# Weighed keys ahead of the next scores: TensorE's order in each step of a streamed attention

## The chip, the cores and the metric

The kernel is written in Bass and runs on one core of a Trainium2 chip. The metric is the device time of one execution in microseconds. All five engines (PE is TensorE, DVE is VectorE, ACT is ScalarE, POOL is GpSimd, SP is SyncE) run their own instruction streams and meet only in semaphores.

## The reference

Three layers with residuals on x of 2 x 256 rows of 512. The change lies in the first, a cross attention of 16 heads over 4096 keys of width 128 in each of the two batches:

```python
x = x + xattn(layernorm(x), ctx_512, ...)     # touched by the change
x = x + attn(layernorm(x), ...)
x = x + ffn(layernorm(x), ...)

# in xattn; kv_r is ctx_512 after rope, one set of keys for all heads of a batch
scores = jnp.einsum('bhsr,bhlr->bhsl', q_r, k_r)
attn = jax.nn.softmax(scores, axis=-1)
ctx_c = jnp.einsum('bhsl,bld->bhsd', attn, kv_r)
```

## The kernel before

**Tiling.** Weights are first folded into the queries, so a query of 128 columns meets the turned keys directly. The attention runs over 64 tiles of queries (2 batches, 16 heads, 2 tiles of 128 rows, `NQT`); each tile meets the 4096 keys in four chunks of 1024 (`NCH`), so there are 256 chunks (`NCHUNK`). To keep float32's precision each operand is split in a high and a low part.

**The life of chunk n.**

- PE, `scores(n)`: six matmuls of 512 columns (lines 1152 to 1154) into one of three slots in PSUM (`slot`, `RING` = 3; two in `ps_s`, one in `ps_t`). `free_slot` waits until the exponents of chunk n-3 have been read out. The last matmul raises `s_done`.
- DVE, `chunk_maximum(n)` (line 864): waits for `s_done`, one maximum over 1024 scores.
- ACT, `exponents(n)` (line 606), then `take_hi(n)` (line 597): exponents in float32, then their high part as float16 into `p_both`; `take_hi` waits for the landing of chunk n-3, whose buffer it takes.
- DVE, `take_lo(n)` (line 856): the low part.
- SP, `turn_exponents(n)` (lines 339 and 340): waits for the end of the weighed keys of chunk n-3 (`pv_done`, the target's buffer) and for `lo_done`, then issues one transposing DMA of both parts (512 KB) from `p_both` to `pt_both`, which raises `pt_in`.
- PE, `weighed_keys(n)`: waits for `pt_in`, then 24 matmuls of 128 columns (lines 1180, 1181, 1184) into `ps_o`.
- DVE, once for each tile: `row_maximum` (line 872) and `weigh_chunks` (line 887), which reads `ps_o`; POOL makes the weights, sums the chunks and splits the next query (`split_query`, lines 444 and 446).

**What sets the order.** Each engine's order is written out by hand. PE does scores 0 to 3 first (`AHEAD` = 4) and then goes through its loop at line 1224. DVE's loop is, for each n: `weigh_chunks` of the tile before (at every fourth n), `chunk_maximum(n + 1)`, `take_lo(n)`, `row_maximum` (at every fourth). ACT's is `exponents(n)`, `take_hi(n)`. SP issues the transposes in order, with a load of later weights (`wmix`) between them once for each 8 chunks of the second half. An engine that waits holds everything behind it in its own stream.

**The turn of the keys.** Batch 1 has other keys. In the four steps ahead of it PE's `next_keys` turns a chunk of 1024 keys through the same three slots (line 1163), and ACT and DVE copy its high and low parts to `kt_hi` and `kt_lo` (lines 612 and 878), in place of the keys of batch 0.

Of the kernel before, what the change touches and what calls it, by code (L numbers as in the profile page):

```python
# [59 lines left out]
def build(nc, x, ctx_kv, wq_t, w_kcq, w_qr_t, w_kr_t, w_kckv, wo_t, cos_q, sin_q, cos_k, sin_k,  # L60
          w_mix, w_gu, w_dn, s_gu, s_dn, out):
    with ExitStack() as stack:
# [969 lines left out]
        def _(pe):  # L1032
# [108 lines left out]
            def scores(n):  # L1141

                k, t, c = RING_AT["chunk", n], n // NCH, n % NCH
                free_slot(k)
                if c == 0:
                    pe.wait_ge(q_ready, t + 1)
                if t % (NQT // B) == 0:
                    pe.wait_ge(kt_done, 8 * (t // (NQT // B)) + 2 * (c + 1))
                for a in range(2):
                    o = slot(k)[:, a, :]  # L1150
                    cols = slice(c * CHUNK + a * HALF, c * CHUNK + (a + 1) * HALF)
                    nc.tensor.matmul(o, q_hi[:, t % 2, :], kt_hi[:, cols], start=True, stop=False)  # L1152
                    nc.tensor.matmul(o, q_hi[:, t % 2, :], kt_lo[:, cols], start=False, stop=False)  # L1153
                    last = nc.tensor.matmul(o, q_lo[:, t % 2, :], kt_hi[:, cols], start=False, stop=True)  # L1154
                last.then_inc(s_done, 1)

            def next_keys(c):

                k = RING_AT["keys", c]
                free_slot(k)  # L1160
                for j in range(CHUNK // P):
                    blk = c * (CHUNK // P) + j
                    last = nc.tensor.transpose(slot(k)[:, j // 4, j % 4 * P:(j % 4 + 1) * P],
                                               kvr[:, 1, blk * P:(blk + 1) * P], ident[:, :])
                last.then_inc(ktt_done, 1)

            def weighed_keys(n):
                b, t, c = n // (NCHUNK // B), n // NCH, n % NCH
                if c == 0 and t >= 2:
                    pe.wait_ge(o_used, t - 1)  # L1170
                if n < NCH:
                    pe.wait_ge(kn_done, 2 * (n + 1))
                elif n == NCHUNK // B:
                    pe.wait_ge(kn_done, KN_DONE)
                o = ps_o[:, t % 2, c * P:(c + 1) * P]
                pe.wait_ge(pt_in[n % RING], 16 * (n // RING + 1))
                pt_hi, pt_lo = pt_both[:, n % RING, 0], pt_both[:, n % RING, 1]
                for k in range(CHUNK // P):
                    keys = slice((c * (CHUNK // P) + k) * P, (c * (CHUNK // P) + k + 1) * P)
                    nc.tensor.matmul(o, pt_hi[:, k, :], kn_hi[b][:, keys], start=(k == 0), stop=False)  # L1180
                    nc.tensor.matmul(o, pt_hi[:, k, :], kn_lo[b][:, keys], start=False, stop=False)  # L1181
                for k in range(CHUNK // P):
                    keys = slice((c * (CHUNK // P) + k) * P, (c * (CHUNK // P) + k + 1) * P)
                    last = nc.tensor.matmul(o, pt_lo[:, k, :], kn_hi[b][:, keys], start=False,  # L1184
                                            stop=(k == CHUNK // P - 1))
                last.then_inc(pv_done, 1)
# [35 lines left out]
            pe.wait_ge(qabs_ok, H)  # L1222
            pe.wait_ge(d_ok, H)
            for n in range(NCHUNK):
                if n + AHEAD < NCHUNK:
                    scores(n + AHEAD)
                if ("keys", n + AHEAD - NCHUNK // B + NCH) in RING_AT:
                    next_keys(n + AHEAD - NCHUNK // B + NCH)
                weighed_keys(n)


            def turn_norm(kind, t):
# [168 lines left out]
```

## Time and profile before

| | us |
|---|---|
| median of 3 runs | 1244.73 |
| lowest and highest | 1244.6, 1246.05 |
| the profiled execution | 1240.12 |
| its span, first to last instruction | 1238.3 |
| PE busy | 1114.0 (90%) |
| DVE busy | 985.4 (80%) |
| ACT busy | 704.3 (57%) |
| POOL busy | 578.0 (47%) |

The span is what the views of the trace divide up; the profiled execution's own time is 1.8 us longer. PE's busy time counts matmuls, which overlap: the end of a row on PE is modelled, and the next matmul starts ahead of it. The distance between starts is therefore the time that a matmul costs. "PEld" is PE's loading of weights. A DMA's start is that of the issuing instruction on SP, and its landing is the last of its 16 engines' signals.

### The profile page before, as it was taken

The numbers are of one execution on the slowest core, as the hardware profiler recorded it, in microseconds if no ns is written. First come the engines' busy times: TensorE is split into PE (matmuls) and PEld (weight loads), VectorE is DVE, ScalarE is ACT, GpSimd is POOL, SyncE is SP. The second block draws the span as 40 slices with busy tenths as digits, with TensorE's granted clock in tenths as the row PEclk, the third lists the DMA queues.
The fourth block names the chain that finished last, engine by engine and source line by source line (L and its number), as shares of the span: only waits on it lengthen the run. The fifth ranks groups of instructions, "written<-read, shape, count | busy, mean of one in ns | idle before, by whom it ended". The sixth has DMA issues, their size and how long they took to land.

```text
span 1238.3 us, 23318 instructions
## 1 busy us (share of the span) xinstructions
PE 1114.0 (90%) x9080; PEld 838.0 (68%) x9080; DVE 985.4 (80%) x930; ACT 704.3 (57%) x1029; POOL 578.0 (47%) x698
## 2 busy tenths in 40 slices
PE   4999997999999999998999999999998869875688
PEld 3555556888888878876787788778787334334567
DVE  4887777899889989887888888888886089996933
ACT  1223236788878878876777777777775031113321
POOL 1993351765766444433344344343442077885200
PEclk9999998999999999999999999999999889987889
DMA  8443305999999999998999999999999200040000
GB/s 303 140 145 99 97 22 105 179 190 183 186 184 191 188 174 190 183 184 163 184 198 186 192 192 196 184 186 191 184 191 163 102 1 0 1 186 1 1 18 17
DMA packets 553990, 175.78 MB, mean 142 GB/s; under 512 B 535072, under 2 KB 541216, under 8 KB 553760
## 3 DMA queue, kind: packets, MB, share of 16 engines
q1 hardware_dynamic: 552272, 169.14, 73.4%
q10 hardware_dynamic: 1616, 5.24, 1.2%
q8 instruction: 69, 1.13, 0.4%
q14 instruction: 33, 0.27, 0.1%
HBM read 39.07 MB, written 1.05 MB: 32 GB/s over the span
## 4 chain that ended last, share of the span: by engine, by line
PE 64%; DMA 19%; DVE 8%; issue 4%; POOL 4%; ACT 2%; DVEq 0%; POOLq 0%; ACTq 0%; SPq 0%
DMA pt_both<-p_both 19%; PE ps_o L1180 7%; PE ps_o L1181 7%; PE ps_o L1184 6%; PE ps_s L1152 5%; PE ps_s L1153 4%; PE ps_s L1154 4%; PE ps_o L1214 3%; PE ps_o L1085 3%; PE ps_s L1060 3%; PE ps_t L1152 2%; POOL prod L517 2%; PE ps_s L1244 2%; PE ps_t L1153 2%; PE ps_t L1154 2%
## 5 line engine op out<-in xcount | busy, mean ns | idle before, releaser
L856 DVE SCALAR_TENSOR_TENSOR p_both<-prob,p_both 128x1024 f16<-128x1024 f32 x256 | 326.4, 1275 | 18.2 <-ACT p_both L597 17.7
L597 ACT ACTIVATE p_both<-prob 128x1024 f16<-128x1024 f32 x256 | 270.6, 1057 | 55.4 <-DMA pt_both<-p_both 37.0
L1180 PE MATMUL ps_o<-kn_hi,pt_both 128*128 128x128 f16 x2048 | 259.0, 220 | 31.6 <-DMA pt_both<-p_both 29.9
L1180 PEld LDWEIGHTS ps_o<-kn_hi,pt_both 128*128 128x128 f16 x2048 | 194.2, 98 | 107.1 <-issue 60.6
L1181 PE MATMUL ps_o<-kn_lo,pt_both 128*128 128x128 f16 x2048 | 256.7, 219 | 0.0
L864 DVE TENSOR_REDUCE nmax<-ps_s 128x1 f32<-128x1024 f32 x172 | 210.2, 1222 | 54.6 <-PE ps_s L1154 52.7
L606 ACT ACTIVATE prob<-ps_s,nmax 128x1024 f32<-128x1024 f32 x172 | 191.7, 1114 | 77.5 <-DVE nmax L864 77.0
L1181 PEld LDWEIGHTS ps_o<-kn_lo,pt_both 128*128 128x128 f16 x2048 | 201.2, 98 | 0.0
L1184 PE MATMUL ps_o<-kn_hi,pt_both 128*128 128x128 f16 x2048 | 156.6, 219 | 0.0
L1152 PE MATMUL ps_s<-kt_hi,q_hi 128*128 128x512 f32 x344 | 150.4, 437 | 4.9 <-DVE kt_lo L878 2.8
L1154 PE MATMUL ps_s<-kt_hi,q_lo 128*128 128x512 f32 x344 | 136.5, 397 | 0.0
L1153 PE MATMUL ps_s<-kt_lo,q_hi 128*128 128x512 f32 x344 | 134.3, 390 | 0.0
L444 POOL CAST q_hi<-arena 128x128 fp32r<-128x128 f32 x64 | 18.8, 293 | 230.2 <-PE ps_s L1154 160.5
L1184 PEld LDWEIGHTS ps_o<-kn_hi,pt_both 128*128 128x128 f16 x2048 | 125.5, 98 | 0.0
L864 DVE TENSOR_REDUCE nmax<-ps_t 128x1 f32<-128x1024 f32 x84 | 102.7, 1223 | 26.3 <-PE ps_t L1154 25.3
L606 ACT ACTIVATE prob<-ps_t,nmax 128x1024 f32<-128x1024 f32 x84 | 93.6, 1114 | 36.5 <-DVE nmax L864 36.3
L469 POOL TENSOR_TENSOR osum<-oscl 128x256 f32<-128x256 f32 x64 | 46.4, 726 | 135.0 <-DVE oscl L887 135.0
L1154 PEld LDWEIGHTS ps_s<-kt_hi,q_lo 128*128 128x128 f32 x344 | 64.8, 188 | 15.2
L1152 PE MATMUL ps_t<-kt_hi,q_hi 128*128 128x512 f32 x168 | 73.5, 438 | 1.4 <-DVE kt_lo L878 1.4
L1152 PEld LDWEIGHTS ps_s<-kt_hi,q_hi 128*128 128x128 f32 x344 | 65.3, 190 | 12.8 <-DVE kt_lo L878 3.2
L453 POOL TENSOR_TENSOR junk<-alpha,rsum 128x4 f32<-128x4 f32 x64 | 65.7, 1027 | 11.6 <-ACT alpha L617 6.6
L1153 PEld LDWEIGHTS ps_s<-kt_lo,q_hi 128*128 128x128 f32 x344 | 65.8, 191 | 7.6
(129 smaller groups left out, 2004.4 us busy)
## 6 DMA issues: line engine op xcount, KB each, us to landing
wgu_raw<-w_gu_dram SPq DMA_DIRECT2D x11, 512.0 KB, 7.5
wq_s<-wq_t_dram SPq DMA_DIRECT2D x16, 256.0 KB, 3.6
wot_s<-wo_t_dram SPq DMA_DIRECT2D x16, 256.0 KB, 2.8
kvr<-ctx_kv_dram ACTq DMA_DIRECT2D x4, 1024.0 KB, 13.7
pt_both<-p_both SPq DMA_TRANSPOSE x256, 4.6
kvr<-w_mix_dram SPq DMA_DIRECT2D x16, 256.0 KB, 3.4
wkcq_s<-w_kcq_dram SPq DMA_DIRECT2D x16, 192.0 KB, 3.0
wdn_raw<-w_dn_dram SPq DMA_DIRECT2D x1, 2816.0 KB, 9.1
```

The lines of the kernel that those rows point to most:

```text
L453: nc.gpsimd.tensor_tensor(junk[:, i, :], alpha[:, i, :], rsum[:, i, :], ALU.mult).then_inc(row_ok, 1)
L469: nc.gpsimd.tensor_tensor(osum[:, :, :], oscl[:, i, 0:2, :], oscl[:, i, 2:4, :], ALU.add).then_inc(ctx_half, 1)
L597: nc.scalar.mul(p_hi(n), prob[:, n % 2, :], PSCALE).then_inc(hi_done, 1)
L606: nc.scalar.activation(prob[:, n % 2, :], scored, ACT.Exp, bias=nmax[:, i, c:c + 1], scale=1.0, accum_out=rsum[:, i, c:c + 1]).then_inc(ex ...
L856: nc.vector.scalar_tensor_tensor(out=p_lo(n), in0=prob[:, n % 2, :], scalar=PSCALE, in1=p_hi(n), op0=ALU.mult, op1=ALU.subtract).then_inc( ...
L864: nc.vector.tensor_reduce(nmax[:, i, c:c + 1], flat(slot(RING_AT["chunk", n])), AX_X, ALU.max, negate=True).then_inc(m_done, 1)
L1152: nc.tensor.matmul(o, q_hi[:, t % 2, :], kt_hi[:, cols], start=True, stop=False)
L1153: nc.tensor.matmul(o, q_hi[:, t % 2, :], kt_lo[:, cols], start=False, stop=False)
L1154: last = nc.tensor.matmul(o, q_lo[:, t % 2, :], kt_hi[:, cols], start=False, stop=True)
L1180: nc.tensor.matmul(o, pt_hi[:, k, :], kn_hi[b][:, keys], start=(k == 0), stop=False)
L1181: nc.tensor.matmul(o, pt_hi[:, k, :], kn_lo[b][:, keys], start=False, stop=False)
L1184: last = nc.tensor.matmul(o, pt_lo[:, k, :], kn_hi[b][:, keys], start=False, stop=(k == CHUNK // P - 1))
```

## The change

In PE's loop over the chunks the call of `weighed_keys(n)` moves from the end of the step to its beginning, ahead of the scores of chunk n+4 and, in the four steps that have them, ahead of the turned keys. Nothing else differs; the waits inside each function stay as they are.

```diff
--- before.py
+++ after.py
@@ -1222,11 +1222,11 @@
             pe.wait_ge(qabs_ok, H)
             pe.wait_ge(d_ok, H)
             for n in range(NCHUNK):
+                weighed_keys(n)
                 if n + AHEAD < NCHUNK:
                     scores(n + AHEAD)
                 if ("keys", n + AHEAD - NCHUNK // B + NCH) in RING_AT:
                     next_keys(n + AHEAD - NCHUNK // B + NCH)
-                weighed_keys(n)
 
 
             def turn_norm(kind, t):
```

## Rows read from the trace of the kernel before

**Rows 1.** The page: busy us (share of the span) xinstructions of each engine.

```profile
PE 1114.0 (90%) x9080; PEld 838.0 (68%) x9080; DVE 985.4 (80%) x930; ACT 704.3 (57%) x1029; POOL 578.0 (47%) x698
```

**Rows 2.** Windows by stage; the columns stand in the first line.

```profile
core 0: us, PE busy (x) PEld busy (x) DVE busy (x) ACT busy (x) POOL busy (x), PEclk, DMA share, GB/s
202.50:956.90 754.40, 722.03 (x7684) 603.15 (x7685) 653.79 (x635) 583.57 (x825) 352.74 (x592) 1.00 1.09 186
```

**Rows 3.** Timeline of PE, 608 to 612 us: start, length, engine, line, operation, count.

```profile
608.42 0.23 PE L1180 MATMUL ps_o<-kn_hi,pt_both 128*128 128x128 f16 x1 [1.12 <-DMA pt_both<-p_both]
...
609.74 0.48 PE L1152 MATMUL ps_t<-kt_hi,q_hi 128*128 128x512 f32 x1
...
610.98 0.40 PE L1154 MATMUL ps_t<-kt_hi,q_lo 128*128 128x512 f32 x1
611.22 0.23 PE L1180 MATMUL ps_o<-kn_hi,pt_both 128*128 128x128 f16 x1
```

**Rows 4.** Waits, 202.5 to 956.2 us, PE and SP's queue: total us, times, longest.

```profile
PE ps_o L1180 <- DMA pt_both<-p_both: 29.9, 37, 3.5
...
SPq L340 <- PE ps_o L1184: 353.2, 231, 2.7
```

**Rows 5.** The chain that ended last, 608 to 633 us: start, us, what.

```profile
613.85 6.35 DMA pt_both<-p_both
620.24 0.23 PE ps_o L1180
...
626.03 6.08 DMA pt_both<-p_both
632.15 0.23 PE ps_o L1180
```

**Rows 6.** Timeline of DVE, 611 to 619 us.

```profile
611.42 1.23 DVE L864 TENSOR_REDUCE nmax<-ps_t 128x1 f32<-128x1024 f32 x1 [0.71 <-PE ps_t L1154]
612.56 1.22 DVE L856 SCALAR_TENSOR_TENSOR p_both<-prob,p_both 128x1024 f16<-128x1024 f32 x1
...
615.35 1.22 DVE L856 SCALAR_TENSOR_TENSOR p_both<-prob,p_both 128x1024 f16<-128x1024 f32 x1
...
618.28 1.46 DVE L856 SCALAR_TENSOR_TENSOR p_both<-prob,p_both 128x1024 f16<-128x1024 f32 x1
```

**Rows 7.** DMA, 202.5 to 956.2 us: queue packets; issues, KB, median us to landing.

```profile
q8 instruction: 60, 0.98, 0.5%
...
pt_both<-p_both SPq DMA_TRANSPOSE x254, 4.6
```

**Rows 8.** DMA, three short windows: from 610.6, from 641.5, from 654.1 us.

```profile
pt_both<-p_both SPq DMA_TRANSPOSE x1, 4.2
...
q8 instruction: 1, 0.02, 4.1%
...
pt_both<-p_both SPq DMA_TRANSPOSE x1, 5.2
...
q8 instruction: 1, 0.02, 11.8%
...
pt_both<-p_both SPq DMA_TRANSPOSE x1, 5.7
```

**Rows 9.** Timeline of PE where the keys turn, 553 to 566 us.

```profile
554.85 0.50 PE L1152 MATMUL ps_t<-kt_hi,q_hi 128*128 128x512 f32 x1 [1.37 <-DVE kt_lo L878]
...
565.39 0.50 PE L1152 MATMUL ps_s<-kt_hi,q_hi 128*128 128x512 f32 x1 [1.44 <-DVE kt_lo L878]
```

**Rows 10.** Windows: 1.5 us behind a landing that came late.

```profile
608.20:609.70 1.50, 1.28 (x23) 1.29 (x24) 0.57 (x2) 1.31 (x2) 0.75 (x2) 1.00 1.24 280
```

**Rows 11.** Windows of two waits of PE, and the end of the second.

```profile
202.90:206.30 3.40, 3.40 (x25) 3.11 (x23) 1.61 (x2) 2.92 (x5) 2.17 (x5) 0.50 1.14 210
583.80:586.80 3.00, 0.01 (x1) 0.00 (x0) 1.23 (x1) 0.02 (x1) 0.00 (x0) 1.00 1.20 218
...
586.81 0.23 PE L1180 MATMUL ps_o<-kn_hi,pt_both 128*128 128x128 f16 x1 [3.00 <-DMA pt_both<-p_both]
```

## The prediction

> **What bounds the kernel now.** I write S(n) for the scores of chunk n (six matmuls) and W(n) for its weighed keys (24 matmuls); there are 256 chunks. The engine table comes first [rows 1]: PE is busy 90% of the span, so one looks for the stretch where it is not. The table by stage puts the change inside one stretch, 202.5 to 956.9 us [rows 2]: 754.4 us, from the start of W(0) to the end of W(255). Less the last W's 1.5 us that is 752.9 us for 255 steps, 2.95 us each. The rest of the kernel is not touched.
>
> PE's own order of time shows what a step costs [rows 3]: W starts at 608.42, the next S at 609.74, the next W at 611.22. W takes 1.32 us, S 1.48 us, together 2.80 us. So 0.15 us of a step is waiting, and the PE waits name the transposing DMA of the exponents, 29.9 us in 37 waits [rows 4]. The chain shows how: a DMA of 6.35 us from 613.85, W at 620.24, then a DMA of 6.08 us and W at 632.15 [rows 5]. With W(137) at 608.42 that is one late landing every 11.8 to 11.9 us, four chunks.
>
> What closes this circle is VectorE's written order: maximum of chunk n+1, then the low half of chunk n. With n = 141: W(137) starts at 608.42; S(142) comes behind it and ends at 610.98 + 0.40 = 611.38, which is 2.96 us later; the maximum of 142 starts at 611.42; the low half of 141 must stand behind it, starts at 612.56 and takes 1.22; the DMA of 141 starts at 613.85 and lands after 6.35; W(141) starts at 620.24 [rows 3, 5, 6]. The sum is 2.96 + 0.04 + 1.14 + 1.22 + 0.07 + 6.35 + 0.04 = 11.82 us, all of the distance. **The circle runs over four chunks because S(n+1) stands behind W(n-4) on PE.**
>
> The DMA of 6.35 us is not the usual one. The median landing takes 4.6 us, and an unhindered one 4.2 us [rows 7, 8]. In this stretch queue 8, instructions, brings 60 packets of 16 KB [rows 7]; PE starts 7684 + 7685 instructions there [rows 2], which is 256 for a packet, one packet each 4.2 chunks (255 / 60). Where a packet falls into a transpose the landing took 5.2 us at 642 and 5.7 us at 654 [rows 8], and the DMAs of 6.35 and 6.08 us meet one late in their flight. I take these as landings held up by an instruction fetch.
>
> **The change part by part.** No instruction, byte or buffer is added or taken away, and PE still needs 2.80 us a step. Only the order moves. Before: S(n+4), W(n). After: W(n), S(n+4), and in the four steps with keys W, S, then the eight transposes of the keys. So every S, and the transposes of keys with it, is now queued behind one more wait for a landing. In terms of circles each loses one chunk of lead: S(n+1) stands behind W(n-3), not W(n-4), and S(n) behind W(n-4), not W(n-5).
>
> Circle one, through VectorE's order, without a fetch: 2.96 + 0.04 + 1.14, the low half 1.28 (three of four take 1.22, the fourth 1.46, [rows 6]), 0.07, a landing of 4.35 (between 4.2 and the median 4.6, nearer the unhindered row, since DMAs will start farther apart), 0.04. That is 9.88 us, now over **three** chunks: 3.29 us a step. Before it was spread over four, 2.47, and bound only with a fetch in it.
>
> Circle two, through the chunk's own work: 2.96 from W to the end of S; from there to the end of the low half 5.19 (S(142) ends at 611.38, its low half at 615.35 + 1.22 = 616.57, [rows 3, 6]), 5.28 on average with the 0.34 us that the fourth chunk has more (0.24 of it the longer low half, 0.10 estimated for its wait behind VectorE's scaling step); 0.07 + 4.35 + 0.04. Sum 12.70 us over four chunks, 3.18 a step without a fetch. But a fetch comes each 4.2 chunks, so this circle can meet nearly all of them. Over 21 chunks lie five fetches: five rounds of 12.70 and one plain PE step of 2.80 give 66.3 us plus five delays.
>
> The delay of a fetch: the rows give 5.2 - 4.35 = 0.85 us when it comes about 2 us into the transpose, 5.7 - 4.35 = 1.35 us later in it, and 6.35 - 4.35 = 2.0 us near its end [rows 5, 8]. The packets come one to two us behind a W's start. After the change a W starts as its own data lands, the next landing is 3.4 us off, so the next DMA was issued 4.35 - 3.4 = 0.95 us before this W: the packet then meets it some 2 to 3 us into its flight. I take the middle of the two rows for that, 1.1 us. (66.3 + 5.5) / 21 = **3.42 us a step**, above both bare circles.
>
> Tested on the kernel before, the same arithmetic gives five rounds of 11.87 and one step, 62.2 / 21 = 2.96, against 2.95 measured.
>
> The turn of the keys: for four chunks an S comes only each 5.3 us (554.85 and 565.39 are two apart, [rows 9]), since keys and scores share three slots. Resource and interval stay, so these four cost 4 x (5.3 - 3.42) = 7.5 us on top of the average after, where they cost 9.4 before.
>
> Sum: 255 x 3.42 + 7.5 = 879.6 us for the stretch, against 752.9: **+126.7 us**. The profiled execution of before took 1240.12 us with a span of 1238.3, and the median of its three runs is 1244.73. So 1366.8 for an execution like the profiled one, and 1371.4 against the median, which I predict.
>
> What else is moved past: W(n) now ends 1.48 us earlier against its S, which frees a buffer of transposed exponents for SP's queue and the accumulator for VectorE. Neither is late: W(138) ends at 611.22 + 1.32 = 612.54, and the DMA that needs its buffer starts only at 613.85, on the low half [rows 3, 5]. With less lead it has still more room. GpSimd's split of the next queries waits for scores and is needed four chunks on; it idles most of the stretch (352.7 of 754.4 us busy, [rows 2]). These cost nothing, and if GpSimd's cover were gone, at most 1.3 us once per four chunks.
>
> **The rivals.** *The fetch is hidden* (the longer step leaves time to catch up): circle one alone, 255 x 3.29 + 8 = 847, +94, **1339 us**. For it: behind a held landing the queue moved 280 GB/s where the stretch had 186 [rows 2, 10], so it can catch up. Against: W(141) and W(145) waited just for such landings. [...]
>
> *Every fetch costs its full 2.0 us*: (66.3 + 10) / 21 = 3.63, +180, **1425 us**.
>
> *The clock falls.* PE will idle 3.42 - 2.80 = 0.6 us a step, 2.6 us a round. [...] Against: behind a wait of 3.00 us at 586.81 the clock stayed 1.00 [rows 11], and my waits are shorter. [...]
>
> *Not slower: the buffer decides.* SP waited 353.2 us in 231 waits for the end of a W before it could issue a transpose [rows 4]. If these released the late DMAs, W ahead of S would issue each 1.48 us sooner and end the 29.9 us of PE's waits: **1215 us**. It decides only where W(n-3) ends later than the low half of n; at 612.54 against 613.78 it doesn't.
>
> *No change: the DMA engines are full.* At a share of 1.09 [rows 2] the order of PE would not matter: **1245 us**. Against: the 280 GB/s of [rows 10] and landings of 4.2 us.
>
> **How the numbers follow.** Forecast 0.70, fetch hidden 0.12, full delay 0.06, clock 0.05, DMA full 0.04, buffer 0.03. Slower by over 0.2%, about what a measurement of this kernel can tell, is then 0.93, same 0.04, faster 0.03. The range takes in the forecast, the hidden fetch with a landing 0.1 us shorter (-9 us) and nearly all of the full delay: 1328 to 1422.
>
> **What would show it.** Right: the stretch from first to last W near 880 us; before nearly each W a wait for the DMA, on PE some 150 us; VectorE's maxima waiting for PE more, its low halves starting 1.14 us behind the next maximum; SP released by the low half instead of W; unhindered landings at 4.2 to 4.5 us; granted clock 1.00. Wrong: landings at a median above 4.6 (the DMA term), a clock of 0.5 in the stretch, or PE's waits unchanged near 30 us, which would mean that the lead was not what bound.

## The result

The changed kernel takes **1411.16 us** in the median of 4 runs (1405.19 to 1415.83) against 1244.66 of the kernel before: a ratio of 1.1337, 95% interval 1.1284 to 1.1391. The forecast of 1371.4 had the way and the mechanism, and the time lies inside its range; the increase was +166.5 us where the sum had +126.7.

The page of the changed kernel, engines and the chain that ended last:

```profile
span 1406.1 us, 23318 instructions
...
PE 1142.8 (81%) x9080; PEld 850.1 (60%) x9080; DVE 979.5 (70%) x930; ACT 707.2 (50%) x1029; POOL 539.7 (38%) x698
...
PE 44%; DMA 30%; DVE 14%; issue 6%; POOL 3%; ACT 1%; SPq 0%; DVEq 0%; POOLq 0%; ACTq 0%
DMA pt_both<-p_both 30%; PE ps_o L1180 5%; DVE p_both L856 4%; PE ps_o L1181 4%; PE ps_o L1184 4%; DVE nmax L864 4%; PE ps_o L1214 3%; PE ps_s L1152 3%; PE ps_o L1085 3%; PE ps_s L1060 3%; PE ps_s L1153 2%; PE ps_s L1154 2%; POOL prod L517 2%; PE ps_s L1244 2%; PE ps_t L1152 1%
```

PE is busy 28.8 us more, though it issues the same instructions; DVE and POOL are busy less, ACT 2.9 us more [rows 1]. The chain of the kernel before had these shares:

```profile
PE 64%; DMA 19%; DVE 8%; issue 4%; POOL 4%; ACT 2%; DVEq 0%; POOLq 0%; ACTq 0%; SPq 0%
```

In the chain the transposing DMA has risen from 19% to 30% of a longer span, and DVE from 8% to 14%, with the low half (L856) and the maximum (L864) at 4% each.

The window from the start of W(0) to the end of W(255), with the columns of [rows 2]; the waits below it are to be read beside [rows 4]:

```profile
202.10:1125.90 923.80, 755.38 (x7690) 618.68 (x7690) 647.58 (x635) 586.41 (x825) 314.21 (x592) 0.98 0.87 152
```

What PE's weighed keys waited for there, us in total, times, longest:

```profile
PE ps_o L1180 <- DMA pt_both<-p_both: 169.9, 129, 5.8
```

And SP's queue, at line 339 for the low half and at line 340 for the buffer:

```profile
SPq L339 <- DVE p_both L856: 329.4, 226, 5.0
SPq L340 <- PE ps_o L1184: 167.2, 138, 3.6
```

The stretch grew from 754.4 to 923.8 us; less the last W it is 922.3 against 752.9 us, +169.4. The two profiled executions took 1407.89 and 1240.12 us, +167.8, so all of the increase lies in the stretch, 3.62 us a step instead of 2.95. PE's wait for landings went from 29.9 us to 169.9 us. SP's queue turned round: it waited 353.2 us for the end of a W and 103.8 for the low half before, and now waits 329.4 for the low half and 167.2 for a W. The buffer did come free earlier, and none of the transposes on the chain waited for it: each was issued behind its low half.

The chain inside the stretch, start, us, what. Each "PE ps_o L1180" of 0.23 us is the start of a W:

```profile
722.27 0.23 PE ps_o L1180
...
725.27 1.23 DVE nmax L864
726.50 1.14 DVE p_both L856
727.71 5.73 DMA pt_both<-p_both
733.48 0.23 PE ps_o L1180
...
736.45 0.07 PE ps_o L1180
...
739.28 1.22 DVE nmax L864
740.50 1.14 DVE p_both L856
741.71 5.87 DMA pt_both<-p_both
747.62 0.23 PE ps_o L1180
```

From 722.27 to 733.48 one sees circle one as the prediction drew it: W(n-3), the S behind it up to 725.27, the maximum, the low half, the DMA, W(n), three chunks in 11.21 us. From 733.48 to 747.62 the chain first takes one plain PE step (the W at 736.45) and then the same circle: four chunks in 14.14 us. Both DMAs, 5.73 and 5.87 us, are held landings.

### The profile page after: what moved, and what is told of

Same layout as the page of the kernel before. It is cut to its first block, busy times and chain, and to the rows that moved or that the text cites. A ratio compares the mean times of both kernels' runs of the same rounds, so it can differ in the third digit from the quotient of the medians.

```text
span 1406.1 us, 23318 instructions
## 1 busy us (share of the span) xinstructions
PE 1142.8 (81%) x9080; PEld 850.1 (60%) x9080; DVE 979.5 (70%) x930; ACT 707.2 (50%) x1029; POOL 539.7 (38%) x698
## 4 chain that ended last, share of the span: by engine, by line
PE 44%; DMA 30%; DVE 14%; issue 6%; POOL 3%; ACT 1%; SPq 0%; DVEq 0%; POOLq 0%; ACTq 0%
DMA pt_both<-p_both 30%; PE ps_o L1180 5%; DVE p_both L856 4%; PE ps_o L1181 4%; PE ps_o L1184 4%; DVE nmax L864 4%; PE ps_o L1214 3%; PE ps_s L1152 3%; PE ps_o L1085 3%; PE ps_s L1060 3%; PE ps_s L1153 2%; PE ps_s L1154 2%; POOL prod L517 2%; PE ps_s L1244 2%; PE ps_t L1152 1%
## 5 line engine op out<-in xcount | busy, mean ns | idle before, releaser
L1180 PE MATMUL ps_o<-kn_hi,pt_both 128*128 128x128 f16 x2048 | 262.7, 222 | 170.1 <-DMA pt_both<-p_both 169.9
L1180 PEld LDWEIGHTS ps_o<-kn_hi,pt_both 128*128 128x128 f16 x2048 | 196.7, 99 | 260.4 <-DMA pt_both<-p_both 170.8
L864 DVE TENSOR_REDUCE nmax<-ps_s 128x1 f32<-128x1024 f32 x172 | 210.4, 1223 | 191.3 <-PE ps_s L1154 190.9
L856 DVE SCALAR_TENSOR_TENSOR p_both<-prob,p_both 128x1024 f16<-128x1024 f32 x256 | 319.6, 1248 | 1.9 <-ACT p_both L597 1.8
L606 ACT ACTIVATE prob<-ps_s,nmax 128x1024 f32<-128x1024 f32 x172 | 191.9, 1116 | 215.2 <-DVE nmax L864 215.2
L1181 PE MATMUL ps_o<-kn_lo,pt_both 128*128 128x128 f16 x2048 | 260.6, 221 | 0.0
L444 POOL CAST q_hi<-arena 128x128 fp32r<-128x128 f32 x64 | 18.9, 295 | 419.1 <-PE ps_s L1154 296.3
L1184 PE MATMUL ps_o<-kn_hi,pt_both 128*128 128x128 f16 x2048 | 160.0, 222 | 0.0
L864 DVE TENSOR_REDUCE nmax<-ps_t 128x1 f32<-128x1024 f32 x84 | 102.7, 1223 | 80.3 <-PE ps_t L1154 79.9
L1152 PE MATMUL ps_s<-kt_hi,q_hi 128*128 128x512 f32 x344 | 154.8, 450 | 4.3 <-DVE kt_lo L878 2.8
L606 ACT ACTIVATE prob<-ps_t,nmax 128x1024 f32<-128x1024 f32 x84 | 93.7, 1116 | 93.4 <-DVE nmax L864 93.4
L1154 PE MATMUL ps_s<-kt_hi,q_lo 128*128 128x512 f32 x344 | 139.4, 405 | 0.0
L1153 PE MATMUL ps_s<-kt_lo,q_hi 128*128 128x512 f32 x344 | 138.0, 401 | 0.0
L1184 PEld LDWEIGHTS ps_o<-kn_hi,pt_both 128*128 128x128 f16 x2048 | 128.4, 100 | 0.0
L1154 PE MATMUL ps_t<-kt_hi,q_lo 128*128 128x512 f32 x168 | 67.0, 399 | 0.0
```

The source lines that it names most:

```text
L606: nc.scalar.activation(prob[:, n % 2, :], scored, ACT.Exp, bias=nmax[:, i, c:c + 1], scale=1.0, accum_out=rsum[:, i, c:c + 1]).then_inc(ex ...
L856: nc.vector.scalar_tensor_tensor(out=p_lo(n), in0=prob[:, n % 2, :], scalar=PSCALE, in1=p_hi(n), op0=ALU.mult, op1=ALU.subtract).then_inc( ...
L864: nc.vector.tensor_reduce(nmax[:, i, c:c + 1], flat(slot(RING_AT["chunk", n])), AX_X, ALU.max, negate=True).then_inc(m_done, 1)
```

## The experiments

In order of what they tell apart. "W first" and "S first" are the orders of the changed kernel and of the one before.

**1. Is it the order or the lead?** W first, with the scores five ahead:

```diff
-AHEAD = 4
+AHEAD = 5
```

> The changed order (weighed keys first), with the scores five chunks ahead instead of four. PE's stream is then chunk by chunk the one of the kernel before. If the lead between scores and weighed keys is what the change cost, the time is that of before, 1245 us (ratio 1.00). If putting a waiting W ahead of S costs by itself (the wait for a landing now stands at the head of the step), it stays near 1411 us.

Measured 1244.51 us, ratio 1.0006 (0.9993 to 1.0019). PE's stream is then the old one again, the turned keys included, so this run shows that the change is nothing else than one chunk of lead taken. What the lead is worth, and on which circle, it can't tell; experiments 2 to 4 and 6 can.

**2. Circle one alone.** PE's order as before, VectorE's maximum two chunks ahead of the low half:

```diff
+taken = 1
 for n in range(NCHUNK):
     ...                                # weigh_chunks, as before
-    if n + 1 < NCHUNK:
-        chunk_maximum(n + 1)
+    two = 1 if NCHUNK // B - NCH - 2 <= n < NCHUNK // B else 2
+    while taken < min(n + 1 + two, NCHUNK):
+        chunk_maximum(taken)
+        taken += 1
     take_lo(n)
```

> PE's order is that of the kernel before; VectorE takes the maximum two chunks ahead of the low half instead of one (one ahead only where the keys turn). Low half n then stands behind S(n+2), which stands behind W(n-3): circle one over three chunks, as in the changed kernel, while the chunk's own path keeps its five chunks of lead (12.70 / 5 = 2.54 us a step, not binding). If circle one is what costs in the changed kernel, this one comes near it: 1371 us by the sum of the prediction, 1411 us as the changed kernel measured. If the lead counts through the chunk's own path, it stays at 1245 us.

Measured 1409.24 us, ratio 1.1328 (1.1301 to 1.1356), the changed kernel's time within the intervals, on PE's old stream. Its page, the costliest PE group (L1183 is L1180 there) and the maximum:

```profile
L1183 PE MATMUL ps_o<-kn_hi,pt_both 128*128 128x128 f16 x2048 | 262.5, 222 | 169.6 <-DMA pt_both<-p_both 169.1
...
L864 DVE TENSOR_REDUCE nmax<-ps_s 128x1 f32<-128x1024 f32 x172 | 210.5, 1224 | 180.1 <-PE ps_s L1157 179.5
```

PE waits 169.1 us for landings, as in the changed kernel (169.9). VectorE's order and PE's order make the same circle, and a chunk of lead taken from it on either side costs the same. This also rules out the chunk's own path, which kept its five chunks here.

**3. Circle two.** The changed kernel with a shorter ScalarE instruction, in circle two and not in circle one:

```diff
-nc.scalar.activation(prob[:, n % 2, :], scored, ACT.Exp, ...)
+m = CHUNK if n < 2 else HALF
+nc.scalar.activation(prob[:, n % 2, 0:m], scored[:, 0:m], ACT.Exp, ...)
```

> The changed kernel; from chunk 2 on the exponents are taken of 512 of the 1024 columns only (the other half keeps old values, so the output is not the attention's). That shortens ScalarE's instruction by about 0.5 us in the chunk's own path (circle two) and leaves circle one alone. If circle two carries the time, a step shortens by 0.5 / 4.2 = 0.12 us, 255 steps 30 us: 1381 us. If circle one carries it, 1411 us, no change.

Measured 1415.45 us, ratio 1.1399 (1.1377 to 1.1421): not shorter at all. ScalarE's larger group of exponents, in the changed kernel (first, from its page) and in this one (in the stretch):

```profile
L606 ACT ACTIVATE prob<-ps_s,nmax 128x1024 f32<-128x1024 f32 x172 | 191.9, 1116 | 215.2 <-DVE nmax L864 215.2
...
L607 ACT ACTIVATE prob<-ps_s,nmax 128x512 f32<-128x512 f32 x169 | 116.2, 688 | 272.5 <-DVE nmax L865 272.5
```

The instruction did shrink, from 1116 to 688 ns, and ScalarE waits for the maximum that much longer.

**4. The low half, which stands in circle one** (and in circle two):

```diff
+m = CHUNK if n < RING else HALF
-nc.vector.scalar_tensor_tensor(out=p_lo(n), in0=prob[:, n % 2, :], ...)
+nc.vector.scalar_tensor_tensor(out=p_lo(n)[:, 0:m], in0=prob[:, n % 2, 0:m], ...)
```

> The changed kernel; from chunk 3 on VectorE takes the low part of 512 of the 1024 columns only (the other half keeps old values, so the output is a little off the attention's). The low half stands in circle one. It gets about 0.6 us shorter, and the chain of the changed kernel passes it 70 times: up to 42 us less, 1369 us. If VectorE's part does not carry the time, it stays at 1411 us, as it did with half the exponents.

Measured 1364.85 us, ratio 1.0961 (1.0931 to 1.0992), 46 us under the changed kernel where 42 were expected. VectorE's group:

```profile
L857 DVE SCALAR_TENSOR_TENSOR p_both<-prob,p_both 128x512 f16<-128x512 f32 x253 | 175.3, 693 | 1.2 <-ACT p_both L597 1.2
```

693 ns instead of 1248: 0.56 us taken from VectorE come back 46 / 0.56 = 83 times over 256 chunks. That is more than the 70 times that the chain passes the low half; in this run the clock also fell less often, four times in the stretch against 11 (the clock's cost is worked out in the next part). ScalarE's 0.43 us came back not once. The two together say that the circle that binds goes through VectorE and past the exponents.

**5. The fetches.** Six wide matmuls in place of 24 narrow ones, in both kernels:

```diff
-for k in range(CHUNK // P):            # 8 x (high, low keys), then 8 more
-    keys = ...
-    nc.tensor.matmul(o, pt_hi[:, k, :], kn_hi[b][:, keys], ...)
-    nc.tensor.matmul(o, pt_hi[:, k, :], kn_lo[b][:, keys], ...)
...
+for j in range(6):
+    keys = slice(c * CHUNK + j % 2 * HALF, c * CHUNK + (j % 2 + 1) * HALF)
+    pt = pt_hi if j < 4 else pt_lo
+    last = nc.tensor.matmul(ps_o[:, t % 2, :], pt[:, j, :], kn_hi[b][:, keys], ...)
```

> The changed kernel; each W's 24 matmuls of 128 columns are replaced by 6 of 512 columns (the same 3072 columns through PE, 24 instructions a chunk instead of 60; the output is not the attention's). W's own time stays near 1.3 to 1.4 us, but PE reads its instructions in 24 packets instead of 60. If the landings held up by instruction fetches are a term of the step, the excess of the landings on the chain (about 75 us in the changed kernel) shrinks to some 30 us: 1411 - 45 + 5 = 1371 us. If the late landings have another cause, it stays at 1411 to 1416 us.

> The same replacement in the kernel before. PE's step is then 2.80 to 2.87 us and 24 fetches are left. If fetches cause the late landings that PE waits for, its 0.15 us of waiting a step goes to under 0.06: 255 x 2.90 = 740 us for the stretch, 12 us less, about 1230 us. If not, 1245 us, or 1260 us by the longer W.

Measured 1364.57 us (ratio 1.0942, 1.0901 to 1.0983) and 1221.53 us (0.9807, 0.9765 to 0.9848). The queue of instructions in the stretch of the first:

```profile
q8 instruction: 25, 0.41, 0.2%
```

PE starts 3078 + 3079 instructions in that stretch (202.0 to 1081.5 us), which is 246 for a packet of 16 KB. In the changed kernel's stretch 7690 + 7690 starts meet 61 packets, 252 for each, so the packets follow PE's instructions down.

And three starts on its PE, S, W, S:

```profile
600.67 0.58 PE L1152 MATMUL ps_s<-kt_hi,q_hi 128*128 128x512 f32 x1
...
602.25 1.47 PE L1181 MATMUL ps_o<-kn_hi,pt_both 128*128 128x512 f16 x6
603.36 0.58 PE L1152 MATMUL ps_t<-kt_hi,q_hi 128*128 128x512 f32 x1
```

From S to S lie 603.36 - 600.67 = 2.69 us, so PE's step got 0.11 us shorter, where I had expected an equal W or a longer one. By estimate that alone is worth 0.11 x 114 = 13 us on the chain of the changed kernel (the 114 is worked out below), which leaves 34 of the 47 us to the fetches and to a clock that fell six times in the stretch instead of 11. In the kernel before, the chain passes W and S 119 times, in this run 161 times, so the shorter step is worth 13 to 18 of the 23 us and 5 to 10 are left to the fetches, against the expected 12; the run alone can't part them.

**6. One more chunk of lead, and one less.** S first with `AHEAD = 5`, and W first with `AHEAD = 3`:

> The kernel before with the scores five ahead instead of four (one more chunk of lead). Circle one then runs over five chunks: with a held landing 11.9 / 5 = 2.4 us a step, below PE's 2.80. If the landings held up by instruction fetches are what PE waits for in the kernel before, these waits go: 255 x 2.80 + 9 = 723 us for the stretch, 30 us less, 1215 us. If another circle takes over (the three buffers of halves: 1.1 + 1.2 + 0.1 + 6.2 = 8.6 us over three chunks, 2.87 a step where a landing is held), it is 1225 to 1240 us. If PE now blocks on a slot of scores in front of W, 1245 us or more.

Measured 1227.43 us, ratio 0.9886 (0.9868 to 0.9903): **faster than both kernels**. The costliest groups of its page:

```profile
L856 DVE SCALAR_TENSOR_TENSOR p_both<-prob,p_both 128x1024 f16<-128x1024 f32 x256 | 327.9, 1281 | 63.5 <-ACT p_both L597 58.6
L597 ACT ACTIVATE p_both<-prob 128x1024 f16<-128x1024 f32 x256 | 270.7, 1057 | 104.0 <-DMA pt_both<-p_both 88.3
L1180 PE MATMUL ps_o<-kn_hi,pt_both 128*128 128x128 f16 x2048 | 258.5, 220 | 19.1 <-DMA pt_both<-p_both 18.9
...
L606 ACT ACTIVATE prob<-ps_s,nmax 128x1024 f32<-128x1024 f32 x172 | 191.0, 1110 | 42.3 <-DVE nmax L864 40.3
L864 DVE TENSOR_REDUCE nmax<-ps_s 128x1 f32<-128x1024 f32 x172 | 209.0, 1215 | 3.6 <-PE ps_s L1154 3.5
```

The maximum hardly waits for PE any more (3.5 us in this group, 52.7 in the kernel before), PE's wait for landings falls to 18.9 us, and a new wait has come in its place: the high half on ScalarE waits 88.3 us for the landing whose buffer it takes (37.0 before), and the low half 58.6 us for the high half. This is the rival written into the expectation, the three buffers of halves. A fourth buffer wasn't tried.

> The changed order with the scores three ahead: one more chunk of lead is taken. Circle one then runs over two chunks: 9.88 / 2 = 4.94 us a step; with five fetches over 21 chunks at 1.1 to 1.5 us each 5.2 to 5.3 us a step, 1330 to 1350 us for the stretch, 1820 to 1840 us in all. If the first chunk of lead was only badly placed and time does not follow the length of the circle, it is far from that, near 1500 us. The clock term grows if PE's longer waits let the clock fall more often: each fall costs up to 1.7 us.

Measured 1967.15 us, ratio 1.5794 (1.5752 to 1.5835). The stretch is 1470.8 us, 5.77 a step: the time follows the circle's length, but the stretch is 121 us above the upper end of what was expected. The 1.7 us of the expectation for a fall is an estimate, half of the 3.4 us that ran at 0.50 from 202.90 us on [rows 11]. One window over the stretch:

```profile
202.00:1690.00 1488.00, 988.21 (x7740) 814.89 (x7738) 647.81 (x639) 589.87 (x831) 270.60 (x594) 0.81 0.50 94
```

The granted clock is 0.81, against 0.98 in the changed kernel's stretch and 1.00 before.

**7. The clock.** The same kernel with work for PE laid into its wait:

```diff
+for k in range(16):
+    nc.tensor.matmul(o, kn_hi[b][:, 0:P], kn_hi[b][:, 0:P], start=True, stop=True)
 pe.wait_ge(pt_in[n % RING], 16 * (n // RING + 1))
```

> The kernel with the scores three ahead (1967 us), where the granted clock was 0.5 for 570 of the stretch's 1471 us and the chain's distance from a W to the end of the next S was 4.73 instead of 2.96 us, 226 us in all over 128 passes. Ahead of each W's wait stand 16 extra matmuls of 128 columns, 0.9 us of work at full clock, whose output W overwrites; PE idles over 2 us a step, so they lie in its wait. If PE's idling lets the clock fall and this carries the excess, the clock stays up and the time falls by up to 226 us, to 1741 to 1790 us, although PE does more. If the clock has nothing to do with the idling, it stays at 1967 us or gets longer.

Measured 1808.86 us, ratio 1.4548 (1.4496 to 1.46), 158 us less, with 4096 matmuls more:

```profile
202.00:1530.00 1328.00, 1016.80 (x11763) 862.36 (x11764) 647.93 (x640) 590.70 (x831) 268.35 (x594) 0.97 0.63 106
```

The clock is back at 0.97. So PE's idling in its waits is what let the clock fall to 0.81 in the run before, and the fall lengthened what follows the wait: there the distance from a W to the end of the next S was 4.73 us in the mean of the chain, here it is 3.17. The gain stays short of 226 us: about 75 of the stretch's 1323 us still ran at the half clock, and late landings stand on the chain again, 57 us over 4.35 us each in 120 landings, where the kernel without the extra matmuls had none (there were also 92 packets of instructions instead of 61, 256 of PE's 11763 + 11764 starts for each).

The maximum over half the columns, the third term of circle one that could be cut (I expected 37 us less), gave no time: without the true maximum some of the halves in `p_both` are no longer finite.

## Why the prediction was right, and where its size was off

To size the terms I followed the chunks' chain back from W(255) in each packed trace: a W that starts within 0.2 us of its landing is followed to its DMA and low half, another W to the S ahead of it on PE; a low half to the maximum or high half that ended last; a maximum to its S; an S to the W ahead of it. 4.35 us is the landing that the prediction took as unhindered. Counts and sums in us:

```
                                  before   changed   2 (VectorE   5 (wide,   W first,
                                             order     two ahead)   changed)   3 ahead
landings on the chain                 45        70          69         77        126
of them through the next maximum      43        69          68         77        125
mean landing                        6.08      5.42        5.54       4.80       4.31
sum of landings over 4.35           77.7      75.0        82.3       34.9       -4.7
W to end of next S, times            119       114         115        100        128
mean of it                          3.01      3.16        3.14       3.00       4.73
```

**What bounds the kernel: right.** In the kernel before 43 of 45 landings of the chain go through VectorE's order, at a mean landing of 6.08 us: the four-chunk circle binds only where a landing is held. That lead is what counts is shown by experiments 2 and 6, that it is VectorE's circle by 2 to 4 and by the trace.

**Circle one over three chunks: right.** 69 of 70.

**Circle two: it carries nothing.** I took its 12.70 us for the path that meets every fetch. The chain does move by four chunks to meet the next fetch, but by circle one and a plain PE step, 9.88 + 2.80 = 12.68 us. That this equals my 12.70 is no chance. The 5.19 us in circle two were read from a row in which the low half of 142 had stood behind the next maximum, so they already held a step of PE and VectorE's order (2.80 + 0.04 + 1.14 + 1.22 = 5.20). The rows of the kernel before beside it:

```profile
614.21 1.23 DVE L864 TENSOR_REDUCE nmax<-ps_s 128x1 f32<-128x1024 f32 x1 [0.44 <-PE ps_s L1154]
...
613.97 1.06 ACT L597 ACTIVATE p_both<-prob 128x1024 f16<-128x1024 f32 x1
```

The chunk's own work had ended with the high half at 613.97 + 1.06 = 615.03, and the low half started at 615.35 [rows 6]. Circle two is thus about 0.3 us shorter than 12.70, and it was circle one under another name: the sum did not suffer, but the path was wrong. In the changed kernel the maximum ends 0.75 us later than the high half in the median of the chain's landings. Experiment 2, which gives the chunk's own path a fifth chunk and still takes 1409 us, and experiment 3 agree.

**The increase**, forecast and measured, on the 255 steps:

```
                                              forecast   from the trace
base: circle one and PE steps                    805       815      70 x 9.88 + 44 x 2.80
held landings                                     67        75
half clock                                         0        18
turn of the keys                                 7.5  \
small waits (landing to W, SP, first chunks)       0  /      14      what is left
stretch                                        879.6     922.3
```

*Base, +10.* I let the chain make 61 rounds, one for a fetch; it makes 70, because where no fetch is near, circle one at 3.29 us a step is longer than a round with a PE step in it, 3.17.

*Held landings, +8.* The term was there and nearly its size: 75 us, and with 25 packets instead of 61 it fell to 35 (experiment 5). About 5 us of both are not a fetch's: the longest landing on the chain, 9.1 us from 671.3 us on, flies beside a load of x of 1024 KB. From the window 671.2 to 671.8 us, issues with the us to landing:

```profile
xres<-x_dram ACTq DMA_DIRECT2D x1, 1024.0 KB, 8.2
pt_both<-p_both SPq DMA_TRANSPOSE x1, 9.1
```

That leaves some 70 us to the fetches, against 67 forecast. In the kernel before, the packets start at 617.97 and 630.24 us, 4.13 us into the DMA of 6.35 us and 4.21 us into that of 6.08. From the window 617.9 to 618.3 us there:

```profile
q8 instruction: 1, 0.02, 18.1%
```

The working of the fetch's delay was wrong in one point. I had the packets meet a transpose 2 to 3 us into its flight and cost 1.1 us. In the trace of the changed kernel most come 2.3 to 3.1 us behind a W's start and 3.8 to 4.4 us into the flight, and there it is all or little: 36 of 50 such landings take 5.7 us or more, mostly up to 6.2, as on the chain above, and 14 take 4.4 to 4.7 us. That the mean came near my 1.1 us a fetch is luck. The changed kernel's packets in the stretch and its median landing, where I had taken 4.35 us for the unhindered one:

```profile
q8 instruction: 61, 1.00, 0.4%
...
pt_both<-p_both SPq DMA_TRANSPOSE x254, 4.4
```

*The clock, +18: the step that failed.* The prediction set it to nothing, since a wait of 3.00 us had left the clock at 1.00 [rows 11] and mine would be shorter. In the changed kernel's stretch the clock fell 11 times: nine times right behind a wait of 1.9 to 2.4 us (there are 20 waits of 1.9 to 2.7 us), once behind one of 4.7 us, at the 9.1 us landing, and once at the end of one of 4.2 us. Two windows, the first with the clock down, the second behind a wait nearly as long that left it up:

```profile
380.60:384.00 3.40, 3.40 (x16) 2.50 (x14) 0.00 (x0) 0.37 (x2) 2.41 (x7) 0.51 1.20 110
...
228.00:231.40 3.40, 2.69 (x30) 2.35 (x30) 1.26 (x1) 2.12 (x3) 0.18 (x1) 1.00 0.79 167
```

PE's timeline where the wait ahead of the first ends, and ahead of the second:

```profile
379.57 0.22 PE L1180 MATMUL ps_o<-kn_hi,pt_both 128*128 128x128 f16 x1 [2.44 <-DMA pt_both<-p_both]
```

```profile
228.71 0.23 PE L1180 MATMUL ps_o<-kn_hi,pt_both 128*128 128x128 f16 x1 [2.15 <-DMA pt_both<-p_both]
```

At 379.57 PE ends a wait of 2.44 us, and from 380.6 the next 3.4 us run at 0.51; at 228.71 it ends one of 2.15 us, and the clock stays at 1.00. The 15 distances from a W to the end of its S that touch such a period are 4.16 us in the mean instead of 2.96, 18 us in all, or 1.6 us a fall, near the 1.7 us that half of the 3.4 us in the row at 202.90 [rows 11] comes to; there were eleven falls, and I had counted none. One wait that had done no harm bounded nothing. In the stretch of W first with three ahead the clock fell 118 times, 570 of 1471 us at the half clock, and experiment 7 shows PE's idling as the cause.

**What a fetch costs.** None of PE's waits in the stretch is for instructions: they are 169.9 us for landings and 4.2 for the turned keys. But the packets hold up transposes that PE then waits for, some 70 us of the changed kernel's stretch. So by PE's own waits the fetch is hidden, as its rival has it, and by the held landings it isn't. With W first and three ahead, no landing on the chain is held (4.31 us in the mean, -4.7 us over 126). Packets meet transposes there too, and 22 landings take over 5.5 us, but all of them belong to the chunks between, since a circle over two chunks passes every other one. So whether a fetch costs hangs on which chunk it falls; why it falls on those wasn't tried.

**The rivals.** The buffer (faster) is out by the result and by SP's issues, each behind a low half on the chain. Full DMA engines (no change) are out: the share fell from 1.09 to 0.87 and the time rose. The hidden fetch (1339 us) is out by the held landings and experiment 5; the full delay (1425 us) lies nearer the result than the forecast does, but not by its mechanism: the held landings cost 75 us, near my 67, and its 122 were not there.

**The signs.** Of what the prediction named as right, PE's waits (169.9 us for 150), the maxima, SP's release and the landings (median 4.4 us) came. Not so the stretch near 880 us, a wait before nearly each W (there are 129 for 256 chunks) and a clock of 1.00; a clock of 0.5 in the stretch stood there as a sign of being wrong, and it was one for the size.

**What was still left.** The split of the last 14 us into keys and small waits is read from the chain and was not tried apart.

## What to carry to other kernels

In a pipeline over several engines, count the chunks of lead around each closed circle of waits, an engine's written order included: a circle's length divided by its chunks is a step, and the longest such quotient is the kernel's pace. Moving one call within a step can take a chunk from every circle that it stands in; here from 9.88 / 4 to 9.88 / 3 us, across PE's own 2.80. The lead taken was paid for in PE's waits for landings (169.9 us in the stretch instead of 29.9), and then in the clock (0.98 instead of 1.00, and 0.81 with another chunk taken). Here adding a chunk (five ahead) gained 1.1% where taking one cost 13%.

## What the runs showed of the hardware

- Packets of 16 KB came on queue 8, instructions, about as often as PE started 250 instructions: 60 for 15369 in the stretch of the kernel before (256 for each), 61 for 15380 in the changed kernel's (252), 25 for 6157 with the wide matmuls (246), 92 for 23527 in experiment 7 (256).
- In the changed kernel 50 landings of the transposing DMA had such a packet start 3.8 to 4.4 us into their flight, and 36 of these took 5.7 us or more; the median of the landings that met no packet was 4.3 us. With 25 packets instead of 61 the landings on the chain lay 35 us above 4.35 us each instead of 75 (experiment 5).
- In the changed kernel's stretch the clock fell to half for 3.4 us behind nine of 20 waits of 1.9 to 2.7 us; its 11 falls cost 1.6 us each in the mean. With W first and three ahead the clock was 0.81; with 4096 matmuls more, laid into PE's waits, it was 0.97 and the time 1808.86 us instead of 1967.15 (experiment 7).
- A step of PE with six matmuls of 512 columns in W took 0.11 us less than one with 24 of 128 and the same columns (2.69 us in experiment 5, 2.80 in the kernel before).
- In the changed kernel a transpose issued at 671.3 us, beside a load of 1024 KB, landed after 9.1 us; the stretch's median landing was 4.4.
